# VectorE's output adds of a fused attention and FFN kernel, each moved into the step of its own product

## The chip, the cores and the metric

The kernel runs on one core of one Trainium2 chip. The metric is the device time of one execution in microseconds (us). Engines: TensorE (PE, matmuls), VectorE (DVE), ScalarE (ACT), GpSimd (POOL), and SyncE (SP), which here issues every DMA.

## The reference

All of it is float32; x is 2048 tokens by 256.

```
xn   = layernorm(x)
k, q, v = W_K xn, W_Q xn, W_V xn          # 16 heads of 128
attn = softmax(causal(q k^T) / sqrt(128))
z    = attn v                              # per head
ffn  = W2 . fwht(silu(W1 xn) * (W3 xn))
out  = x + W_O concat(z) + ffn
```

## The kernel before

The FFN and the values of all heads come first (about the first 300 us). Then the attention runs head by head, 16 times the same period of 8 steps; heads 1 to 14 are one loop body, heads 0 and 15 are written out, and a last stretch called `over` drains what is left. Each engine has its own program; the order of its work is written out by hand, and semaphores tie the engines together.

Every float32 product is made of three matmuls on a high and a low part (`_hi`, `_lo`) of each operand (L811 to L813). ScalarE copies the high part out of PSUM, and VectorE (for pt and v: GpSimd) subtracts it to get the low part.

**One step s.** A step treats two rows of 128 queries, the big one (row 15 - s) and the small one (row s); together they have 17 blocks of 128 keys. TensorE computes `scores` into PSUM banks 0 to 4. VectorE's `maxima` (L715 to L726) takes the maxima bank by bank. ScalarE's `exponential` (L529) writes exp(scores - max) to `raw` in three pieces, two of the big row and one of the small. VectorE's `transpose_blocks` (L733) transposes `raw` in 32x32 blocks, the big row first, then the small one. SP's `send` writes each row to `scratch` in DRAM with four DMAs (L275), and `bring` fetches it transposed into `pt_lo` (L289). Two steps later ScalarE's `p_to_hi` (L538) and GpSimd's `p_to_lo` (L371) split it.

**z and its output.** A chunk z of 256 queries needs the rows of two steps. TensorE's `weighted_sum` gathers it in bank 7. ScalarE copies it (`z_to_hi`, L544), VectorE subtracts (`z_to_lo`, L737), and TensorE's `output` multiplies it by W_O into one of two ring banks. VectorE's `output` (L749) then does two `scalar_tensor_tensor` of 128x256: acc = product x 1/(row sum) + acc. The ring is shared with the projections of K and Q (`kq_to_lo`, L697 and L700), in the fixed order `ITEMS`; TensorE may overwrite a bank once the reader of the item before in it is done (for an output: `out_added`).

The output chunks are numbered 0 to 7. Even steps 0, 2, 4, 6 carry the small ones (`O_SMALL`: chunks 3, 5, 7 of the head before, and 1), odd steps 1, 3, 5, 7 the big ones (`O_BIG`: chunks 4 and 6 of the head before, and 0 and 2). TensorE's order is: in an even step `scores`, small `output`, big `weighted_sum`; in an odd step `scores`, big `weighted_sum`, big `output`, small `weighted_sum`; the projections stand between them.

VectorE's order in an even step: `z_to_lo` of the small chunk, the adds of the big chunk of the step before, both `maxima`, `reciprocals`, big transpose, small transpose, `kq_to_lo`. In an odd step: the adds of the small chunk of the step before, both `maxima`, `z_to_lo` of the big chunk, big transpose, small transpose, `kq_to_lo`.

Of the kernel before, what the change touches and what calls it, by code (L numbers as in the profile page):

```python
# [18 lines left out]
def attention_ffn_kernel(nc, x, w_heads, w_values, w1t, w3t, w2t, hadamard, out):  # L19
# [19 lines left out]
    STEPS = TILES // 2  # L39
# [27 lines left out]
    O_SMALL = {0: (-1, 3), 2: (-1, 5), 4: (-1, 7), 6: (0, 1)}  # L67
    O_BIG = {1: (-1, 4), 3: (-1, 6), 5: (0, 0), 7: (0, 2)}
# [24 lines left out]
    with ExitStack() as ctx:  # L93
# [122 lines left out]
        def wait(engine, semaphore, count):  # L216

            if not isinstance(count, int) or count > 0:
                engine.wait_ge(semaphore, count)

        def kq_count(h, item):

            return 8 * h + KQ_FIRST + KQ_ITEMS.index(item) + 1
# [4 lines left out]
        def z_count(h, z):  # L228

            return CHUNKS * h + z + 1  # L230
# [363 lines left out]
        def _(dve):  # L594
# [94 lines left out]
            def ring_bank(item):  # L689
                return bank(RING_AT + ITEM[item] % RING)  # L690

            def kq_to_lo(h, item):
                which, b = item
                sl = slice(b * BANK, (b + 1) * BANK)
                dve.wait_ge(proj_hi, kq_count(h, item))
                if which == "K":
                    dve.tensor_tensor(k_lo[:, sl], ring_bank(item), k_hi[:, sl].bitcast(F32),  # L697
                                      ALU.subtract).then_inc(proj_lo, 1)
                else:
                    dve.scalar_tensor_tensor(out=q_lo[:, sl], in0=ring_bank(item), scalar=SCALE,  # L700
                                             in1=q_hi[:, sl].bitcast(F32), op0=ALU.mult,
                                             op1=ALU.subtract).then_inc(proj_lo, 1)

            def maxima(h, s, small):

                j = row_of(s, small)
                at = big_banks(s) if small else 0
                end = STEP_BANKS if small else big_banks(s)
                parts = [(b, b + 1) for b in range(at, end)]
                if not small:  # L710
                    parts[0:2] = [(0, 2)]
                for i, (a, b) in enumerate(parts):
                    n = min((b - a) * BANK, (j + 1) * P - (a - at) * BANK)
                    scores = ps[:, a * BANK:a * BANK + n]
                    dve.wait_ge(scored, STEP_BANKS * (STEPS * h + s) + b)  # L715
                    if b == end:
                        dve.memset(wait_mark[:, :], 0.0)
                        dve.tensor_tensor_reduce(  # L718
                            out=scores, in0=scores, in1=mask[:, BANK - n:], scale=1.0,
                            scalar=-3e38, op0=ALU.add, op1=ALU.max, accum_out=bank_max[:, j, i:i + 1]  # L720
                        ).then_inc(maxed, 1)
                    else:
                        dve.tensor_reduce(bank_max[:, j, i:i + 1], scores, AX_X, ALU.max).then_inc(maxed, 1)  # L723

                dve.wait_ge(maxed, 4 * (STEPS * h + s) + (4 if small else len(parts)))
                dve.tensor_reduce(neg_max[:, j:j + 1], bank_max[:, j, 0:len(parts)], AX_X, ALU.max,  # L726
                                  negate=True).then_inc(negmaxed, 1)

            def transpose_blocks(h, s, small):

                dve.wait_ge(exped, piece_count(h, s, 2 if small else 1))
                v = raw_row(s, small).rearrange("p (b k) -> p b k", k=BLK)
                dve.transpose(v, v).then_inc(blocked, 1)  # L733

            def z_to_lo(h, z):
                dve.wait_ge(z_hi_done, z_count(h, z))
                dve.tensor_tensor(z_lo[:, :], bank(Z, 0, CHUNK_Q), z_hi[:, :].bitcast(F32),  # L737
                                  ALU.subtract).then_inc(z_lo_done, 1)

            def output(h, z):  # L740

                c = Z_ORDER[z]
                dve.wait_ge(rcp_done, z_count(h, z))
                dve.wait_ge(wo_product, z_count(h, z))

                wait(dve, out_added, z_count(h, z) - 1)
                for t in range(2):
                    j = 2 * c + t
                    ins = dve.scalar_tensor_tensor(  # L749
                        out=acc[:, j, :], in0=ring_bank(("O", z))[:, t * D:(t + 1) * D], scalar=row_rcp[:, j:j + 1],  # L750
                        in1=acc[:, j, :], op0=ALU.mult, op1=ALU.add)
                ins.then_inc(out_added, 1)

            def reciprocals(h, m):

                dve.wait_ge(exped, piece_count(h, 2 * m + 1, 2))
                j, i = 2 * (CHUNKS - 1 - m), 2 * m
                dve.tensor_reduce(row_sum[:, j:j + 2], row_part[:, j:j + 2, :], AX_X, ALU.add).then_inc(summed, 1)
                dve.wait_ge(summed, CHUNKS // 2 * h + m + 1)
                dve.reciprocal(row_rcp[:, j:j + 2], row_sum[:, j:j + 2]).then_inc(rcp_done, 1)  # L760
                dve.reciprocal(row_rcp[:, i:i + 2], row_part[:, i:i + 2, 0]).then_inc(rcp_done, 1)

            def period(h, first=False, more=True, over=False):
                def absent(back):
                    return first and back or over and not back

                for s in range(6 if over else STEPS):
                    if s in O_SMALL and not absent(O_SMALL[s][0]):
                        z_to_lo(h + O_SMALL[s][0], O_SMALL[s][1])

                    back, z = (O_SMALL if s % 2 else O_BIG)[(s - 1) % STEPS]
                    if s == 0:
                        back -= 1
                    if not absent(back):
                        output(h + back, z)
                    if not over:
                        maxima(h, s, 0)
                        maxima(h, s, 1)
                    if s % 2 == 0 and not (first and s == 0) and not (over and s > 0):
                        reciprocals(*((h, s // 2 - 1) if s else (h - 1, 3)))  # L780
                    if s == 7 and more:
                        kq_to_lo(h, ("K", 0))
                    if s in O_BIG and not absent(O_BIG[s][0]):
                        z_to_lo(h + O_BIG[s][0], O_BIG[s][1])
                    if not over:
                        transpose_blocks(h, s, 0)
                    if s == 7 and more:
                        kq_to_lo(h, ("K", 1))
                    if not over:
                        transpose_blocks(h, s, 1)  # L790
                    if s < 2 and not over:
                        kq_to_lo(h, ("Q", s + 1))
                    if s == 3 and more and not over:
                        kq_to_lo(h, ("K", 3))
                    if s >= 5 and more and not over:
                        kq_to_lo(h, (("Q", 3), ("Q", 0), ("K", 2))[s - 5])

            dve.wait_ge(mask_ready, 2)
            for item in KQ_ITEMS[2:]:
                kq_to_lo(-1, item)  # L800
            period(0, first=True)
            with dve.Fori(1, HEADS - 1) as h:
                period(h)
            period(HEADS - 1, more=False)
            period(HEADS, over=True)

# [274 lines left out]
```

## Time and profile before

| what | value |
|---|---|
| median of 3 runs | 1470.24 us (1469.47 to 1470.25) |
| the profiled execution | 1468.4 us |
| its span, first to last instruction | 1466.5 us |
| mean granted TensorE clock | 0.983 of full speed |
| busy: PE, DVE, ACT, POOL | 1350.7, 1048.4, 836.4, 838.5 us |
| period of one head in the loop | 72.28 us |

The profiled execution took 1.8 us less than the median. The period is the distance of the same instruction in successive heads. Times below are us from the start of the span. In a timeline the first column is the start, the second the duration; durations of neighbours on an engine overlap a little, so what an instruction costs its engine is better read from the distance of two starts.

### The profile page before, as it was taken

To read this page: it belongs to the slowest core of one execution; us is meant where nothing else is said; L and a number is where in the kernel's file an instruction comes from. 1 tells how busy PE (TensorE), PEld (TensorE's weight loads), DVE (VectorE), ACT (ScalarE), POOL (GpSimd) and SP (SyncE) were. 2 spreads that over 40 slices of the span, in tenths; PEclk is the share of its full clock that TensorE was granted. 3 is DMA by queue.
4 is the path that set the end of the run, shared out by engine and by line. 5 is a ranking of instruction groups with operands and counts; after the bars stand their busy time and mean duration, and the time that the engine had idled before them with its cause. 6 is when DMAs were issued, how large, how long until landed. Compare 5 with 4: busy or idle time off the path is not lost.

```text
span 1466.5 us, 26458 instructions
## 1 busy us (share of the span) xinstructions
PE 1350.7 (92%) x8104; PEld 1189.0 (81%) x8104; DVE 1048.4 (71%) x2389; ACT 836.4 (57%) x1623; POOL 838.5 (57%) x532
## 2 busy tenths in 40 slices
PE   3999999969999999999999999999999999999986
PEld 2878888758888888888888888888888888888875
DVE  6643300378888888888888888888888888888882
ACT  3322244366666666666666666666666666666662
POOL 4410000065757585858585857576767676767574
PEclk7899999989999999999999999999999999999998
DMA  4100056589897978888888887978898888888885
GB/s 145 68 1 0 0 151 194 157 249 284 256 284 250 283 244 282 246 284 260 276 254 281 248 286 253 283 252 284 251 281 247 281 262 264 271 261 271 263 266 167
DMA packets 278458, 335.13 MB, mean 229 GB/s; under 512 B 62736, under 2 KB 251280, under 8 KB 273808
## 3 DMA queue, kind: packets, MB, share of 16 engines
q1 hardware_dynamic: 278416, 334.65, 73.1%
q8 instruction: 17, 0.28, 0.1%
q14 instruction: 25, 0.20, 0.0%
HBM read 173.08 MB, written 161.48 MB: 228 GB/s over the span
## 4 chain that ended last, share of the span: by engine, by line
PE 27%; issue 26%; POOL 24%; DVE 8%; ACT 6%; DMA 4%; SPq 4%; POOLq 1%; DVEq 0%; ACTq 0%
POOL pt_lo L371 21%; PE ps L811 9%; PE ps L812 9%; PE ps L813 9%; SPq L275 3%; DMA scratch<-raw 3%; ACT raw L529 3%; DVE had L723 3%; ACT pt_hi L538 1%; POOL v_lo L376 1%; DVE raw L733 1%; POOL wqk_lo L355 1%; DMA raw<-w3t 1%; DVE acc L749 1%; POOL wqk_hi L353 1%
## 5 line engine op out<-in xcount | busy, mean ns | idle before, releaser
L371 POOL TENSOR_TENSOR pt_lo<-pt_lo,pt_hi 128x640 fp32r<-128x640 f32 (+11 forms) x384 | 662.0, 1756 | 241.7 <-ACT pt_hi L538 241.7
L529 ACT ACTIVATE raw<-ps,had 128x1024 f32<-128x1024 f32 (+7 forms) x384 | 329.2, 865 | 323.0 <-DVE had L726 263.3
L733 DVE STREAM_TRANSPOSE raw<-raw 128x2048 f32<-128x2048 f32 (+15 forms) x256 | 322.0, 1292 | 94.5 <-ACT raw L529 92.3
L811 PE MATMUL ps<-pt_hi,v_hi 128*128 128x256 f32 (+1 forms) x1152 | 324.6, 282 | 20.7 <-POOL pt_lo L371 19.1
L812 PE MATMUL ps<-pt_lo,v_hi 128*128 128x256 f32 (+1 forms) x1152 | 329.6, 286 | 0.0
L813 PE MATMUL ps<-pt_hi,v_lo 128*128 128x256 f32 (+1 forms) x1152 | 327.5, 284 | 0.0
L538 ACT CAST pt_hi<-pt_lo 128x640 fp32r<-128x640 f32 (+11 forms) x384 | 282.3, 812 | 12.0 <-DMA pt_lo<-scratch 11.9
L811 PE MATMUL ps<-k_hi,q_hi 128*128 128x512 f32 (+3 forms) x640 | 238.2, 372 | 18.5 <-ACT raw L529 18.4
L723 DVE TENSOR_REDUCE had<-ps 128x1 f32<-128x1024 f32 (+1 forms) x256 | 237.9, 950 | 8.1 <-PE ps L813 8.1
L811 PEld LDWEIGHTS ps<-pt_hi,v_hi 128*128 128x128 f32 x1152 | 219.8, 191 | 29.6 <-issue 21.8
L813 PE MATMUL ps<-k_hi,q_lo 128*128 128x512 f32 (+3 forms) x640 | 233.9, 365 | 0.0
L812 PE MATMUL ps<-k_lo,q_hi 128*128 128x512 f32 (+3 forms) x640 | 233.3, 365 | 0.0
L812 PEld LDWEIGHTS ps<-pt_lo,v_hi 128*128 128x128 f32 x1152 | 219.1, 190 | 2.9
L813 PEld LDWEIGHTS ps<-pt_hi,v_lo 128*128 128x128 f32 x1152 | 221.5, 192 | 0.0
L376 POOL TENSOR_TENSOR v_lo<-v_next,v_hi 128x512 fp32r<-128x512 f32 x64 | 82.7, 1303 | 223.4 <-ACT v_hi L513 223.4
L811 PEld LDWEIGHTS ps<-k_hi,q_hi 128*128 128x128 f32 x640 | 121.2, 189 | 41.1 <-ACT raw L529 23.3
L813 PEld LDWEIGHTS ps<-k_hi,q_lo 128*128 128x128 f32 x640 | 120.9, 189 | 19.3
L812 PEld LDWEIGHTS ps<-k_lo,q_hi 128*128 128x128 f32 x640 | 121.3, 190 | 17.9
L737 DVE TENSOR_TENSOR z_lo<-ps,z_hi 128x256 fp32r<-128x256 f32 x128 | 54.2, 424 | 102.7 <-ACT z_hi L544 102.7
L718 DVE CUSTOM_DVE_ANT_0 ps<-ps,aux 128x512 f32<-128x512 f32 (+3 forms) x256 | 126.8, 495 | 0.0
L811 PE MATMUL ps<-wo_hi,z_hi 128*128 128x256 f32 x256 | 79.3, 310 | 43.6 <-DVE z_lo L737 41.6
L697 DVE TENSOR_TENSOR k_lo<-ps,k_hi 128x512 fp32r<-128x512 f32 x64 | 42.5, 664 | 101.8 <-ACT k_hi L489 101.8
(101 smaller groups left out, 2202.8 us busy)
## 6 DMA issues: line engine op xcount, KB each, us to landing
all_values<-raw SPq DMA_DIRECT2D x16, 1024.0 KB, 5.0
v_next<-all_values SPq DMA_DIRECT2D x16, 1024.0 KB, 5.4
scratch<-raw SPq DMA_DIRECT2D x64, 256.0 KB, 5.4
pt_lo<-scratch SPq DMA_DIRECT2D x16, 1024.0 KB, 5.5
scratch<-raw SPq DMA_DIRECT2D x64, 240.0 KB, 5.2
pt_lo<-scratch SPq DMA_DIRECT2D x16, 960.0 KB, 6.1
scratch<-raw SPq DMA_DIRECT2D x64, 224.0 KB, 5.4
pt_lo<-scratch SPq DMA_DIRECT2D x16, 896.0 KB, 5.0
```

What stands on the lines that cost most here:

```text
L275: sp.dma_start(to[a], raw_row(s, small)[a * BLK:(a + 1) * BLK].rearrange("k (g x) -> k g x", g=4)).then_inc(stored[small], 16)
L371: pool.tensor_tensor(lo, lo.bitcast(F32), hi.bitcast(F32), ALU.subtract).then_inc(pt_lo_done, 1)
L376: pool.tensor_tensor(v_lo[:, sl], v_next[:, sl], v_hi[:, sl].bitcast(F32), ALU.subtract).then_inc(v_lo_done, 1)
L529: act.activation(to[:, first // P:(first + n) // P], ps[:, a * BANK:a * BANK + n].rearrange("p (i g k) -> p i g k", g=4, k=BLK), ACT.Exp, ...
L538: act.copy(pt_row(pt_hi, j, a, b), pt_row(pt_lo, j, a, b).bitcast(F32)).then_inc(pt_hi_done, 1)
L718: dve.tensor_tensor_reduce(out=scores, in0=scores, in1=mask[:, BANK - n:], scale=1.0, scalar=-3e38, op0=ALU.add, op1=ALU.max, accum_out=ba ...
L723: dve.tensor_reduce(bank_max[:, j, i:i + 1], scores, AX_X, ALU.max).then_inc(maxed, 1)
L733: dve.transpose(v, v).then_inc(blocked, 1)
L737: dve.tensor_tensor(z_lo[:, :], bank(Z, 0, CHUNK_Q), z_hi[:, :].bitcast(F32), ALU.subtract).then_inc(z_lo_done, 1)
L811: pe.matmul(dst, a[0], b[0], start=start, stop=False, skip_group_check=True)
L812: pe.matmul(dst, a[0], b[1], start=False, stop=False, skip_group_check=True)
L813: return pe.matmul(dst, a[1], b[0], start=False, stop=stop, skip_group_check=True)
```

## The change

Only VectorE's order changes. The adds of a small chunk go from the start of the next (odd) step to the even step of their product, between the transposes of the big and of the small row. The adds of a big chunk go from the next (even) step, where they stood behind `z_to_lo`, to the end of their own odd step, behind both transposes and `kq_to_lo`. The last stretch `over` needs five steps in place of six. No operation is added or taken away.

```diff
-                for s in range(6 if over else STEPS):
+                for s in range(5 if over else STEPS):
                     if s in O_SMALL and not absent(O_SMALL[s][0]):
                         z_to_lo(h + O_SMALL[s][0], O_SMALL[s][1])
-
-                    back, z = (O_SMALL if s % 2 else O_BIG)[(s - 1) % STEPS]
-                    if s == 0:
-                        back -= 1
-                    if not absent(back):
-                        output(h + back, z)
                     if not over:
                         maxima(h, s, 0)
                         maxima(h, s, 1)
...
                         transpose_blocks(h, s, 0)
                     if s == 7 and more:
                         kq_to_lo(h, ("K", 1))
+                    if s in O_SMALL and not absent(O_SMALL[s][0]):
+                        output(h + O_SMALL[s][0], O_SMALL[s][1])
                     if not over:
                         transpose_blocks(h, s, 1)
...
                         kq_to_lo(h, (("Q", 3), ("Q", 0), ("K", 2))[s - 5])
+                    if s in O_BIG and not absent(O_BIG[s][0]):
+                        output(h + O_BIG[s][0], O_BIG[s][1])
```

## Rows read from the trace of the kernel before

**Rows 1.** The page, part 1: busy time of each engine.

```profile
PE 1350.7 (92%) x8104; PEld 1189.0 (81%) x8104; DVE 1048.4 (71%) x2389; ACT 836.4 (57%) x1623; POOL 838.5 (57%) x532
```

**Rows 2.** Busy time by stretch: PE, PEld, DVE, ACT, POOL, clock, DMA share, GB/s.

```profile
374.00:446.00 72.00, 68.25 (x433) 60.93 (x432) 59.62 (x139) 46.56 (x92) 49.78 (x33) 1.00 0.87 270
```

**Rows 3.** Waits from 390 to 1380 us: total, times, longest.

```profile
ACT raw L529 <- DVE had L726: 213.5, 91, 4.0
...
PE ps L811 <- DVE z_lo L737: 24.7, 26, 1.5
PE ps L811 <- POOL pt_lo L371: 12.9, 18, 0.9
...
PE ps L811 <- ACT raw L529: 8.8, 13, 0.7
```

**Rows 4.** Timeline of TensorE, one head; in brackets idle before, and releaser.

```profile
783.53 0.28 PE L813 MATMUL ps<-wo_hi,z_lo 128*128 128x256 f32 x1
...
785.03 0.45 PE L811 MATMUL ps<-k_hi,q_hi 128*128 128x512 f32 x1
...
786.24 0.39 PE L813 MATMUL ps<-k_hi,q_lo 128*128 128x512 f32 x1
...
799.57 0.38 PE L811 MATMUL ps<-wo_hi,z_hi 128*128 128x256 f32 x1 [0.46 <-DVE z_lo L737]
...
809.56 0.50 PE L811 MATMUL ps<-k_hi,q_hi 128*128 128x512 f32 x1 [0.68 <-ACT raw L529]
...
817.23 0.39 PE L811 MATMUL ps<-wo_hi,z_hi 128*128 128x256 f32 x1 [1.43 <-DVE z_lo L737]
...
825.77 0.38 PE L811 MATMUL ps<-pt_hi,v_hi 128*128 128x256 f32 x1 [0.88 <-POOL pt_lo L371]
...
1315.54 0.50 PE L811 MATMUL ps<-k_hi,q_hi 128*128 128x512 f32 x1 [0.68 <-ACT raw L529]
```

**Rows 5.** Timeline of VectorE, same head: steps 0, 1 to 2, 2 to 3.

```profile
785.73 0.42 DVE L737 TENSOR_TENSOR z_lo<-ps,z_hi 128x256 fp32r<-128x256 f32 x1 [1.23 <-ACT z_hi L544]
...
786.86 1.81 DVE L723 TENSOR_REDUCE had<-ps 128x1 f32<-128x1024 f32 x2
...
804.59 0.42 DVE L737 TENSOR_TENSOR z_lo<-ps,z_hi 128x256 fp32r<-128x256 f32 x1 [0.73 <-ACT z_hi L544]
804.93 0.87 DVE L749 SCALAR_TENSOR_TENSOR acc<-ps,had,acc 128x256 f32<-128x256 f32 x2
805.72 1.81 DVE L723 TENSOR_REDUCE had<-ps 128x1 f32<-128x1024 f32 x2
...
810.42 2.50 DVE L733 STREAM_TRANSPOSE raw<-raw 128x1792 f32<-128x1792 f32 x2 [1.14 <-ACT raw L529]
812.85 0.83 DVE L749 SCALAR_TENSOR_TENSOR acc<-ps,had,acc 128x256 f32<-128x256 f32 x2
813.61 1.81 DVE L723 TENSOR_REDUCE had<-ps 128x1 f32<-128x1024 f32 x2
```

**Rows 6.** Timelines of ScalarE (two rows) and GpSimd (one), same head.

```profile
808.30 1.11 ACT L529 ACTIVATE raw<-ps,had 128x1024 f32<-128x1024 f32 x1 [3.74 <-DVE had L726]
...
819.58 2.22 ACT L538 CAST pt_hi<-pt_lo 128x960 fp32r<-128x960 f32 x3
...
819.78 1.31 POOL L376 TENSOR_TENSOR v_lo<-v_next,v_hi 128x512 fp32r<-128x512 f32 x1 [2.66 <-ACT v_hi L513]
```

**Rows 7.** SP: waits from 374 to 1382 us, timeline, page's part 6.

```profile
SPq L289 <- PE ps L813: 20.6, 25, 1.8
...
811.29 1.19 SPq L289 DMA_DIRECT2D pt_lo<-scratch  x2
812.57 6.64 SPq L275 DMA_DIRECT2D scratch<-raw  x8
821.07 0.97 SPq L289 DMA_DIRECT2D pt_lo<-scratch  x2
...
pt_lo<-scratch SPq DMA_DIRECT2D x16, 960.0 KB, 6.1
```

## Prediction

> **What bounds the kernel now.** The page first: TensorE is busy for 92% of the span, VectorE for 71% [rows 1]. That is a mean over stages, so the second view is the busy time by stretch. In 72 us of a middle head, TensorE works 68.25 us at a granted clock of 1.00, that is at the 2.4 GHz level, while VectorE works 59.62 us [rows 2]. So at most 72 - 68.25 = 3.75 us of a head are idle time that a better order could remove. The waits of the middle heads say who ends them [rows 3]: TensorE waits for `z_lo` of VectorE (26 times), for `pt_lo` of GpSimd (18) and for the exponentials (13), about 25, 13 and 9 us over some 14 heads.
>
> The timeline of one head places these gaps [rows 4]: 0.46 us at 799.57 (big output of step 1, for `z_lo`), 0.68 at 809.56 (scores of step 3, for the exponentials), 1.43 at 817.23 (big output of step 3, for `z_lo`) and 0.88 at 825.77 (`weighted_sum` of step 4, for `pt_lo`), together 3.45 us. From there to the next head TensorE runs on almost without a gap. The period is (1315.54 - 809.56) / 7 = 72.28 us, the same for all loop heads.
>
> A head therefore has two halves. From step 4 to step 0 TensorE sets the pace. From step 0 to step 4 the path leaves it: VectorE's maxima, ScalarE's exponentials, VectorE's transposes, then maxima again. The exponential of step 2 starts after 3.74 us of waiting for VectorE's negated maximum [rows 6], and such waits hold 213.5 us over these heads [rows 3]. What makes the maxima of steps 0 to 3 start earlier shortens the head, until TensorE has no gaps left.
>
> **The price of one pair of adds.** By starts, 805.72 - 804.93 = 0.79 us [rows 5]. In the order before, the big pair stands between `z_to_lo` and the maxima of steps 0, 2, 4 and 6, the small pair in front of the maxima of steps 1, 3, 5 and 7.
>
> **The big pair, step 1 to 2.** It goes in front of `z_to_lo` of step 2, where VectorE is idle for 0.73 us, waiting for ScalarE's `z_hi` [rows 5]. The next instruction starts 0.08 us before the reported end of the adds (804.93 + 0.87 against 805.72), so the hole is 0.81 us wide by starts and the pair fits with 0.02 to spare. Its cover is ScalarE's cast; were the cover gone, it would cost its 0.79 again. The maxima of step 2 then follow `z_to_lo` directly, at its start + 0.34, and gain the whole 0.79 us. The lower bound is 0.65, if the adds had to end by their reported end (0.87 - 0.73 = 0.14 late); the upper is 0.79.
>
> **The big pair, step 7 to 0.** The hole in front of `z_to_lo` is 1.23 us, so the pair is covered. The maxima at 786.86 could start at 785.73 + 0.34 = 786.07. But they read two banks of scores, whose last matmul starts at 786.24 and takes 0.39 [rows 4, 5]: 786.63, and some hundredths for the hand-over. Gain 0.2 us, between 0 and 0.23. After that the scores are late next, and they are TensorE's own pace.
>
> **The big pairs, steps 3 to 4 and 5 to 6.** They too leave the front of the maxima. But behind 825.77 TensorE has no gap that VectorE ends until the next head [rows 4], so nobody is waiting for that time: 0, between 0 and a few tenths.
>
> **The small pairs.** Before step 3, the order was big transpose, small transpose, adds, maxima: 810.42, then 812.85 for the adds, then 813.61 for the maxima, with no idle time between them [rows 5]. Now it is big transpose, adds, small transpose, maxima. The sum in front of the maxima is the same, so they gain nothing. What moves is the end of the small transpose, 0.79 us later, and in steps 0 and 6 the Q subtraction behind it. SP issues the small row's four DMAs behind the big row's four; the eight take 6.64 us [rows 7], so the small ones begin some 3.3 us after 812.57, and the small transpose would now end near 812.92 + 0.79 = 813.7 against 815.9. Price 0. The cover is the big row's four issues.
>
> **New waits.** A pair now waits for a product of its own step. In step 7, the tightest, TensorE's product ends at 783.53 + 0.28 = 783.81, and VectorE comes free at 785.73 - 1.23 = 784.50 [rows 4, 5]. In step 1 the product begins at 799.57 and VectorE comes free at 804.59 - 0.73 = 803.86. Behind a late product would stand `z_to_lo` of the next step, and behind it TensorE's small output; I price this at 0. The ring banks come free earlier than before, but none of TensorE's gaps names them.
>
> **How the gain travels.** Step 0 brings 0.2, so exponentials, transposes and maxima of step 1 are 0.2 earlier, and the gap at 799.57 closes by 0.2. Step 2 adds 0.79: the exponential at 808.30 comes 0.99 earlier. TensorE's gap of 0.68 at 809.56 closes, since TensorE itself comes only 0.2 earlier. The chain goes on through the transposes at 810.42 and the maxima at 813.61 to `z_lo`, so the output at 817.23 is 0.99 earlier; its gap only shrinks to about 1.3 because TensorE also arrives 0.2 + 0.68 earlier. ScalarE's exponentials and v cast, and GpSimd's `v_lo` at 819.78, idle 2.66 us before it [rows 6], move too, and with them `pt_lo` and the matmul at 825.77. From there on all is TensorE's pace: a period of 72.28 - 0.99 = 71.3 us.
>
> SP must follow. The row of step 1 is fetched at 811.29, its 960 KB take 6.1 us to land, and ScalarE casts it at 819.58 [rows 6, 7]: 2.2 us of slack, of which about 0.8 is used up, since the fetch moves only by the 0.2 of step 0. SP also waits for TensorE 20.6 us in these heads [rows 7], so it is not the slowest loop.
>
> **The sum.** Big pairs of 15 heads do this (head 0 has no outputs in its first steps; head 15's first four steps have the same order): 15 x 0.99 = 14.9 us. The last stretch changes nothing I can price. The profiled execution would take 1468.4 - 14.9 = 1453.5; the median is 1.8 higher, so 1470.2 - 14.9 = 1455.4 us. With the bounds of the two terms, 15 x (0.65 + 0) = 9.8 to 15 x (0.79 + 0.23) = 15.3, and up to 0.2 a head for what steps 4 to 6 might add: 1452 to 1461 for this case.
>
> **The rivals.**
>
> *Another gate takes most of it* (0.14). VectorE's hole of step 1 is filled to 0.02 us, the DMA engines are busy for 0.87 of the time [rows 2], and the fetched row keeps 1.4 us of slack. If a wait of ScalarE for a fetched row, or of SP for a landing, takes two thirds, 5 us remain: 1465. For it: several reserves shrink at once. Against it: each is still positive.
>
> *VectorE's order is not what costs* (0.12). The same time, 1470.2. For it: VectorE has 12 us of a head idle, and TensorE is the busiest engine. Against it: three of TensorE's four gaps end at VectorE or at work behind its maxima.
>
> The Trainium skill, Perfetto Trace Analysis, section Identifying the Most-Contended Engine, would have the engine of highest occupancy optimized first, and VectorE isn't that one. By that rule the sum would be 0 and the time this rival's. This case's waits [rows 3] speak against it, as just said.
>
> *Slower: the small transpose is late for SP* (0.06). In one even step SP has finished the big row's issues before the small transpose ends, and the loop of fetch, split and `weighted_sum` hangs on it. Its price is 0.79 us in one step of 15 heads, with no gain got: 1470.2 + 11.9 = 1482. It decides from the point where the small row's first DMA is now issued less than 0.79 us after its transpose; the trace has about 3 us [rows 5, 7].
>
> *More than the forecast* (0.06): the maxima of steps 4 and 6 count as well and TensorE's gaps close further, 1.5 us a head: 1448.
>
> **How the numbers follow.** Forecast 0.62, 1455.4 us. Faster by over 0.2% (2.9 us, about what a measurement of this kernel can tell from no change): forecast, most of the first rival and the last one, 0.81; within 0.2%: 0.12; slower: 0.07. The range of 1450 to 1465 holds the forecast with its bounds and most of the partial case, and leaves out no change, slower, and more than 20 us.
>
> **What would show it.** Right: a period near 71.3 us; the adds inside the hole before `z_to_lo` in step 2, so that its idle time falls from 0.73 to about 0; maxima of step 2 starting 0.34 us after `z_to_lo`; TensorE's gap before the scores of step 3 gone, the one at the output of step 3 still near 1.3 and the one at step 4 near 0.9. Wrong: idle time of VectorE in front of the adds (the product late), or ScalarE idle before `p_to_hi` for a DMA, or SP idle for a small transpose.

## The result, and the profile after

The changed kernel takes 1457.14 us (median of 4, 1454.75 to 1457.69) against 1470.05 before (median of 4): ratio 0.991, 95% interval 0.9893 to 0.9927. Forecast were 1455.4 us and a gain of 14.9 us; measured is a gain of 12.9. The profiled execution took 1454.75 us, 13.65 less than the one before; the other three took about 2.5 us longer than it.

The period of a loop head fell from 72.28 to 71.32 us. The output of step 3 begins at 454.62 and, five heads on, at 811.22: 356.60 / 5 = 71.32. The timeline of TensorE of the changed kernel, the same gaps as in [rows 4]:

```profile
454.62 0.39 PE L809 MATMUL ps<-wo_hi,z_hi 128*128 128x256 f32 x1 [1.44 <-DVE z_lo L737]
...
794.33 0.38 PE L809 MATMUL ps<-wo_hi,z_hi 128*128 128x256 f32 x1 [0.29 <-DVE z_lo L737]
...
811.22 0.39 PE L809 MATMUL ps<-wo_hi,z_hi 128*128 128x256 f32 x1 [1.44 <-DVE z_lo L737]
...
819.73 0.39 PE L809 MATMUL ps<-pt_hi,v_hi 128*128 128x256 f32 x1 [0.88 <-POOL pt_lo L371]
```

The gap of 0.46 us is now 0.29, the one of 0.68 before the scores of step 3 is gone, and those of 1.43 and 0.88 are still there: 3.45 us became 2.61. This accounts for 0.84 of the 0.95 us that a head is shorter (the remaining 0.1 us is taken up further below). Busy time by stretch, to hold against [rows 2], has TensorE at 69.14 of 72 us:

```profile
374.00:446.00 72.00, 69.14 (x440) 61.92 (x439) 60.70 (x144) 47.17 (x93) 50.74 (x33) 1.00 0.86 265
```

The timeline of VectorE of the changed kernel, step 0, then steps 1 to 3, answers to [rows 5]:

```profile
780.66 0.42 DVE L737 TENSOR_TENSOR z_lo<-ps,z_hi 128x256 fp32r<-128x256 f32 x1 [0.45 <-ACT z_hi L544]
781.60 1.82 DVE L723 TENSOR_REDUCE had<-ps 128x1 f32<-128x1024 f32 x2 [0.51 <-PE ps L811]
...
793.77 0.42 DVE L737 TENSOR_TENSOR z_lo<-ps,z_hi 128x256 fp32r<-128x256 f32 x1
...
798.53 0.86 DVE L749 SCALAR_TENSOR_TENSOR acc<-ps,had,acc 128x256 f32<-128x256 f32 x2
799.36 0.42 DVE L737 TENSOR_TENSOR z_lo<-ps,z_hi 128x256 fp32r<-128x256 f32 x1
799.70 1.81 DVE L723 TENSOR_REDUCE had<-ps 128x1 f32<-128x1024 f32 x2
804.40 2.05 DVE L733 STREAM_TRANSPOSE raw<-raw 128x1792 f32<-128x1792 f32 x1 [1.14 <-ACT raw L529]
806.37 0.83 DVE L749 SCALAR_TENSOR_TENSOR acc<-ps,had,acc 128x256 f32<-128x256 f32 x2
807.12 0.57 DVE L733 STREAM_TRANSPOSE raw<-raw 128x384 f32<-128x384 f32 x1
807.62 1.78 DVE L723 TENSOR_REDUCE had<-ps 128x1 f32<-128x1024 f32 x2
```

In step 0 the adds have gone from between `z_lo` and the maxima, but the maxima now wait 0.51 us for scores: `z_lo` to maxima is 0.94 us, before it was 786.86 - 785.73 = 1.13, a gain of 0.19. In step 2 the adds fill the hole of 0.73 us, `z_lo` follows with no idle time, and the maxima start 0.34 us after it; before it was 1.13, a gain of 0.79. Before step 3 the small pair stands between the two transposes, and from the first transpose to the maxima it is 807.62 - 804.40 = 3.22 us, against 813.61 - 810.42 = 3.19 before.

SP, in its waits and its timeline, against [rows 7]:

```profile
SPq L289 <- PE ps L811: 8.3, 16, 1.2
SPq L275 <- DVE raw L733: 2.4, 5, 1.2
...
805.96 1.19 SPq L289 DMA_DIRECT2D pt_lo<-scratch  x2
807.24 6.59 SPq L275 DMA_DIRECT2D scratch<-raw  x8
```

The small transpose of step 2 ends at 807.69; the eight issues begin at 807.24 and take 6.59 us, so the small row's four come about 3 us later. SP's waits for a transpose are 2.4 us in all, so the later small transpose holds it up very little. SP's waits for TensorE fell from 20.6 us to 8.3: it is closer to being late.

### The profile page after: what moved, and what is told of

Same layout as the page of the kernel before. It is cut to its first block, busy times and chain, and to the rows that moved or that the text cites. A ratio compares the mean times of both kernels' runs of the same rounds, so it can differ in the third digit from the quotient of the medians.

```text
span 1452.9 us, 26444 instructions
## 1 busy us (share of the span) xinstructions
PE 1350.0 (93%) x8104; PEld 1189.3 (82%) x8104; DVE 1051.3 (72%) x2389; ACT 837.1 (58%) x1623; POOL 838.6 (58%) x532
## 4 chain that ended last, share of the span: by engine, by line
POOL 32%; issue 31%; PE 24%; DVE 6%; ACT 3%; DMA 2%; SPq 1%; POOLq 1%; DVEq 0%; ACTq 0%
POOL pt_lo L371 27%; PE ps L809 8%; PE ps L810 8%; PE ps L811 8%; POOL v_lo L376 2%; ACT raw L529 2%; DVE had L723 1%; DVE raw L733 1%; POOL wqk_lo L355 1%; DMA raw<-w3t 1%; POOL wqk_hi L353 1%; SPq L275 1%; DVE k_lo L636 1%; POOL wo_lo L355 1%; DMA scratch<-raw 1%
## 5 line engine op out<-in xcount | busy, mean ns | idle before, releaser
L733 DVE STREAM_TRANSPOSE raw<-raw 128x2048 f32<-128x2048 f32 (+15 forms) x256 | 328.6, 1299 | 94.6 <-ACT raw L529 92.0
L538 ACT CAST pt_hi<-pt_lo 128x640 fp32r<-128x640 f32 (+11 forms) x384 | 282.3, 811 | 13.3 <-DMA pt_lo<-scratch 13.1
L749 DVE SCALAR_TENSOR_TENSOR acc<-ps,had,acc 128x256 f32<-128x256 f32 x256 | 108.4, 464 | 6.0 <-PE ps L811 5.2
```

The costliest lines, as they stand in the source:

```text
L538: act.copy(pt_row(pt_hi, j, a, b), pt_row(pt_lo, j, a, b).bitcast(F32)).then_inc(pt_hi_done, 1)
L749: ins = dve.scalar_tensor_tensor(out=acc[:, j, :], in0=ring_bank(("O", z))[:, t * D:(t + 1) * D], scalar=row_rcp[:, j:j + 1], in1=acc[:, j ...
```

## The experiments

Besides each run's time stands the period, read as the distance of step 3's `z_lo` in successive loop heads of its profile.

| kernel | median us | ratio to before (95%) | period us |
|---|---|---|---|
| before | 1469.7 to 1470.1 | | 72.28 |
| changed | 1457.1 | 0.9910 (0.9893 to 0.9927) | 71.33 |
| e1_big_only | 1456.2 | 0.9914 (0.9897 to 0.9930) | 71.33 |
| e2_small_only | 1470.5 | 1.0004 (0.9994 to 1.0014) | 72.28, the first 73.41 |
| e3_big_step1 | 1458.7 | 0.9931 (0.9914 to 0.9947) | 71.48 |
| e4_big_step7 | 1466.6 | 0.9979 (0.9970 to 0.9989) | 72.07 |
| e5_big_steps35 | 1469.2 | 0.9997 (0.9988 to 1.0006) | 72.26 |
| e6_small_in_hole | 1448.3 | 0.9847 (0.9826 to 0.9868) | 70.14, some 70.8 to 72.8 |
| e7_z_lo_early | 1459.4 | 0.9936 (0.9922 to 0.9950) | 71.3, one of 71.7, three near 72.8 |
| e8_both | 1458.1 | 0.9919 (0.9904 to 0.9934) | 71.57, single 70.1, 70.7 and 73.4 |
| e9_v_cast_early | 1445.6 | 0.9846 (0.9831 to 0.9860) | 70.48, some 70.7 to 71.5 |
| e10_small_and_v | 1446.8 | 0.9843 (0.9829 to 0.9856) | 69.3 to 74.6 |

**Which pairs carry the gain.** Four kernels take the change apart. e1, the small pairs left where they were:

```diff
-                    if not absent(back):
+                    if s % 2 and not absent(back):
                         output(h + back, z)
...
+                    if s in O_BIG and not absent(O_BIG[s][0]):
+                        output(h + O_BIG[s][0], O_BIG[s][1])
```

> Only the big pairs are added in their own step; the small pairs stay at the start of the next odd step. Theory (the gain is the big pairs leaving the front of the maxima of steps 0 and 2): period 71.3 us and a time within 3 us of the full change, about 1457. Rival (small pairs carry part of it, by the ring banks that come free earlier or by the odd steps' maxima): period above 71.6, gain clearly smaller.

e2, the reverse:

```diff
-                    if not absent(back):
+                    if s % 2 == 0 and not absent(back):
...
+                    if s in O_SMALL and not absent(O_SMALL[s][0]):
+                        output(h + O_SMALL[s][0], O_SMALL[s][1])
                     if not over:
                         transpose_blocks(h, s, 1)
```

> Only the small pairs are moved, between the two transposes; the big pairs stay behind the next step's z subtraction. Theory: the sum of work in front of the odd steps' maxima is unchanged, period 72.3 us, time 1470 within 2 us. Rival 1 (the later small transpose delays SP's sends): up to 0.79 us a head slower, period 73.1, 1482. Rival 2 (the small move helps by itself): period below 72.1.

The big pairs alone give the whole gain, the small ones nothing, neither way. In 13 of 14 loop heads of e2 the later small transpose costs nothing, so the slower rival falls. The first loop head is 1.13 us longer; ScalarE waits there for two fetched rows (0.49 and 1.23 us), and whether the later transpose is the cause isn't shown.

e3, e4 and e5 move only the big pairs of step 1, of step 7, and of steps 3 and 5 (shown is e3):

```diff
+                    if (s % 2 or (s - 1) % STEPS not in (1,)) and not absent(back):
...
+                    if s in (1,) and not absent(O_BIG[s][0]):
+                        output(h + O_BIG[s][0], O_BIG[s][1])
```

> Only the big pair of step 1 is added in its own step, everything else as before the change. Theory: it brings 0.79 us in front of the maxima of step 2; period 71.5 us, time 1470.1 - 15 x 0.79 = 1458. Rival (the gain is spread over all four big pairs): about a quarter of it, period 72.0, 1467.

> Only the big pair of step 7 is added in its own step. Theory: the maxima of step 0 gain 0.2 us until the scores are late; period 72.1 us, time 1470.1 - 3 = 1467. Rival (all pairs count alike): 0.24 to 0.8 us a head, the upper end 1458.

> Only the big pairs of steps 3 and 5 are added in their own steps. Theory: behind step 4 TensorE sets the pace and nobody waits for that time; period 72.3 us, time 1470 within 2 us. Rival (these pairs count too): up to 1.5 us a head faster, 1448.

Step 1's pair brings 72.28 - 71.48 = 0.80 us a head, step 7's 0.21, those of steps 3 and 5 0.02. That settles the division: 0.80 and 0.21 against the forecast 0.79 and 0.2. Together they give 0.95 rather than 1.01; where the last 0.06 goes was not traced.

**Does the chain from step 0 to 3 set the period?** e6 puts the small pairs where VectorE waits for ScalarE:

```diff
+                    if s in O_SMALL and not absent(O_SMALL[s][0]):
+                        output(h + O_SMALL[s][0], O_SMALL[s][1])
                     if not over:
                         transpose_blocks(h, s, 0)
...
-                    if s in O_SMALL and not absent(O_SMALL[s][0]):
-                        output(h + O_SMALL[s][0], O_SMALL[s][1])
                     if not over:
                         transpose_blocks(h, s, 1)
```

> The changed kernel, but the small pairs stand in front of the big row's transpose, where VectorE waits for ScalarE (1.56 us in step 0, 1.14 in step 2), and not behind it. Theory (what counts is the work of the VectorE and ScalarE chain from step 0 to step 3, and a hole before the transpose is free): the maxima of step 3 come 0.79 us earlier; in step 0 about 0.3 us more, until ScalarE's cast of z is late for the first exponential of step 1; period 71.3 - 1.1 = 70.2 us, time 1457 - 16 = 1441. Rival 1 (another gate, SP or the fetched rows, is close behind): period 70.8 or more. Rival 2 (only the order of the big pairs matters): 71.3.

Half a hit: the period is 70.14 us in most heads, 1.19 less than with the change, but five loop heads are longer (70.79 to 72.77 us), and the median of 1448.3 (1442.5 to 1451.7) is 7 us above the forecast. The rival of another gate holds for those: in each of the five, ScalarE waits 0.92 to 1.97 us for the fetched row of step 1. The timeline of ScalarE of e6 in the longest shows it, and under it TensorE's, of the head before and of this one:

```profile
807.75 2.20 ACT L538 CAST pt_hi<-pt_lo 128x960 fp32r<-128x960 f32 x3 [1.45 <-DMA pt_lo<-scratch]
```

```profile
742.20 0.38 PE L809 MATMUL ps<-pt_hi,v_hi 128*128 128x256 f32 x1 [0.94 <-POOL pt_lo L371]
...
813.50 0.38 PE L809 MATMUL ps<-pt_hi,v_hi 128*128 128x256 f32 x1 [1.72 <-POOL pt_lo L371]
```

ScalarE waits 1.45 us for the fetched row of step 1, and TensorE's gap at step 4 grows from 0.94 to 1.72. Counted from `z_lo` of step 3, the `weighted_sum` of step 4 begins after 10.14 us in this head and after 9.06 in the head before. That is 1.1 of the 2.6 us by which this head is longer than 70.14. The rest stands behind the gap, where busy time by stretch shows a granted clock (third column from the end) below 1.00, in this loop head of e6 only:

```profile
813.50:830.00 16.50, 16.50 (x100) 15.44 (x101) 12.27 (x28) 10.99 (x23) 12.23 (x10) 0.90 0.84 269
```

What makes the fetched row late is argued and not shown. SP waits for TensorE only 0.4 us in all these heads, which fits a loop of sends and fetches that has become the pace, but no run made that loop shorter.

**Is TensorE's largest gap worth closing?** In step 3, e7 subtracts z between the two maxima, on top of the change; e8 does so on top of e6:

```diff
                     if not over:
                         maxima(h, s, 0)
+                    if s == 3 and not absent(O_BIG[s][0]):
+                        z_to_lo(h + O_BIG[s][0], O_BIG[s][1])
+                    if not over:
                         maxima(h, s, 1)
...
-                    if s in O_BIG and not absent(O_BIG[s][0]):
+                    if s in (1, 5, 7) and not absent(O_BIG[s][0]):
```

> The changed kernel, but in step 3 VectorE subtracts the big z between the maxima of the two rows, so that TensorE's largest gap (1.44 us at the output of step 3) becomes shorter by about 1.3 us. Theory: the chain through ScalarE's v cast and GpSimd's splits still ends at the same time, so that TensorE waits that much longer at step 4's weighted sum; period 71.3, time 1457 within 2. Rival (TensorE's largest gap is what its idle time costs): period 70.0, time 1438.

> Small pairs in front of the big transpose, and the big z of step 3 subtracted between the maxima of the two rows. Theory: as with the small pairs alone, period 70.2, since the second edit shortens a gap that is not on the path. Rival: with the chain shorter, TensorE's own gap at the output of step 3 binds, and both together give 69.5 or less.

e7: the gap at step 3's output falls to 0.48 us, the one at step 4 grows from 0.88 to 1.78, and the period stays 71.3, as the theory has it. But three of its heads are about 1.45 us longer, and its 1459.4 us lie just outside the forecast of 1457 within 2. In e8 nearly all are longer: 71.57 in place of the 70.2 expected, a miss of both theories. Its timeline of TensorE at step 4, first a head of period 70.08, then one of 71.56:

```profile
1175.84 0.39 PE L812 MATMUL ps<-pt_hi,v_hi 128*128 128x256 f32 x1 [1.82 <-POOL pt_lo L371]
...
1176.19 0.29 PE L814 MATMUL ps<-pt_hi,v_lo 128*128 128x256 f32 x1
1176.31 0.28 PE L812 MATMUL ps<-pt_hi,v_hi 128*128 128x256 f32 x1
...
531.54 0.38 PE L812 MATMUL ps<-pt_hi,v_hi 128*128 128x256 f32 x1 [1.74 <-POOL pt_lo L371]
...
534.93 0.41 PE L812 MATMUL ps<-pt_hi,v_hi 128*128 128x256 f32 x1
535.15 0.41 PE L813 MATMUL ps<-pt_lo,v_hi 128*128 128x256 f32 x1
```

Behind the second gap, the matmuls start 0.22 us apart and no longer 0.12. Busy time by stretch of e8, for the 13.5 us behind either gap:

```profile
1175.80:1189.30 13.50, 13.46 (x91) 12.53 (x92) 10.40 (x23) 10.39 (x23) 10.71 (x9) 1.00 0.88 275
...
531.50:545.00 13.50, 13.46 (x83) 12.73 (x84) 9.26 (x23) 9.29 (x20) 9.46 (x8) 0.87 0.90 285
```

TensorE is busy for 13.46 us in both stretches, yet in the second the mean granted clock is 0.87, so part of it ran at 1.2 GHz and not at 2.4. By the clock alone this would be about 0.13 x 13.5 = 1.8 us (an estimate from this row); the two periods differ by 71.56 - 70.08 = 1.48 us, and e7's three heads by about 1.45.

So moving 1 us of idle time from one gap into another made the kernel slower. The two gaps of 1.44 and 0.88 us of the changed kernel are followed by no lower clock in any loop head. One gap of 1.71 to 1.82 us was followed by it in 11 of 14 loop heads of e8. But one of 1.72 to 1.83 us was followed by it in only 3 of 14 of e7, and of the two heads shown the one with the longer gap kept its clock. The length of the gap alone doesn't decide, and no run shows what does. The Trainium skill, Perfetto Trace Analysis, section Matmul Optimizations, says that TensorE scales its power by utilization and that matmuls should run back to back in batches; the row with 0.87 agrees, the row with 1.00 behind a gap as long doesn't show it.

**The way into step 4.** e9 leaves VectorE as changed and moves ScalarE's v cast of step 3 to the start of the step:

```diff
+                    if s == 3 and not over:
+                        v_to_hi(h, 2)
                     if s in (1, 3) and not absent(O_BIG[s][0]):
                         z_to_hi(h + O_BIG[s][0], O_BIG[s][1])
...
-                    for b in [] if over else V_AT.get(s, []):
+                    for b in [] if over or s == 3 else V_AT.get(s, []):
```

> The changed kernel, but ScalarE casts the v block of step 3 at the start of the step, in an idle time of 1.4 us, instead of behind the exponentials. Theory (the path into step 4's weighted sum runs through ScalarE's v cast and GpSimd's two splits, not through TensorE's output gap of step 3): the gap of 0.88 us at the weighted sum closes and the period falls from 71.33 to about 70.5 us, 1445. Rival (the fetched row of step 1 or SP's loop is close behind): ScalarE then waits for the fetched row, and the period stays above 70.9.

A hit: 70.48 us and 1445.6. From its waits between 390 and 1360 us:

```profile
PE ps L811 <- DVE z_lo L739: 22.8, 27, 1.5
...
PE ps L811 <- POOL pt_lo L371: 3.6, 10, 1.0
```

TensorE's waits for `pt_lo` fell to 3.6 us, from 12.9 before the change [rows 3] and 13.1 in the changed kernel, while the larger ones for `z_lo` stayed. In five of the 14 loop heads the period is 0.2 to 1.0 us longer, and in four of these ScalarE waits 0.4 to 0.9 us for a fetched row: the rival holds in part.

e10 joins e6 and e9.

> The small pairs in front of the big transposes and the early v cast together. Theory (the fetched row of step 1 is now the gate, since SP's loop of sends and fetches leaves ScalarE waiting up to 2 us in some heads): little beyond the small pairs alone, 70.1 us where the row is in time, with some longer heads, 1440 to 1449. Rival (the chain through ScalarE and GpSimd still sets it): 69.3 us, 1433. A third outcome, from the runs before: a gap of TensorE longer than about 1.5 us at step 4 is followed by a lower granted clock and costs about 1.4 us more in that head.

The median lies within the theory's 1440 to 1449 and is e9's within the intervals. By heads it is neither alone: the fastest reach the rival's 69.3, others 70.5 to 74.6. The third outcome came too, in the heads of 72.3 and 74.6 us: behind gaps of 1.62 and 1.72 us at step 4 the granted clock falls to 0.66 and 0.50 over 5 us. It is no rule, though, for e7 has gaps up to 1.83 us without it. Its waits of ScalarE and SP, where the changed kernel has 0.9 and 8.3:

```profile
ACT pt_hi L538 <- DMA pt_lo<-scratch: 19.8, 16, 2.6
...
SPq L289 <- PE ps L813: 1.4, 2, 0.8
```

In the four heads of 69.0 to 69.4 us ScalarE doesn't wait for the fetched row of step 1, in the other ten it waits 0.7 to 2.6 us for it: the fetched rows are now what binds. e6, e9 and e10 all beat both kernels, the one before by 1.5%, the changed one by 0.6 to 0.8%; among them this study doesn't separate a best one, though e9 varies least (1445.3 to 1449.8).

## Why the prediction was right

- **What bounds the kernel:** right. From step 0 to 4 the path runs through VectorE and ScalarE; shortening it shortened every head, and time saved behind step 4 (e5) was worth 0.02 us. One reading the prediction left out: the profile puts 59.7 us of the exponentials' waits down to the landing of a send and not to the maxima. The landing didn't hold those of steps 0 and 1: in e4, where only the big pair of step 7 moved, they came 0.19 us earlier with the maxima, counted from the start of step 4.
- **Big pair, step 1 to 2:** forecast 0.79 us, 0.79 in the timeline, 0.80 alone in e3. The hole of 0.73 us held the pair.
- **Big pair, step 7 to 0:** forecast 0.2, 0.19 in the timeline, 0.21 in e4; then the scores were late, as said.
- **Small pairs:** forecast 0, e2 0.00 us in 13 of 14 heads. The cover by the big row's four issues held.
- **New waits for a product:** no idle time stands in front of any pair in any loop head, only in the last stretch from 1419.68 us on (0.80 to 1.80 us). From the output of step 3 of head 15 (1394.98 before, 1381.40 after) to the end it is 71.5 us in both kernels, so the last stretch is worth nothing, as priced.
- **TensorE's gaps:** the scores' gap closed and that of step 4 stayed, as said. The gap of step 3 was to be 1.3 and is 1.44. The first matmul after the gap at 809.56 starts 0.33 us ahead of the next (809.56 to 809.89), others 0.23, and that 0.1 us went with the gap, so TensorE arrives 0.1 earlier at the next one; the sum had left it out.
- **The sum:** mis-sized by a little. Forecast 0.99 us a head, measured 0.95 to 0.96: 15 heads give 14.4. The profiled execution gained 13.65, because its head 0 stood 0.55 us later than before's already in its first scores, before any output, and 0.12 us more by the end of head 0. The other three executions are some 2.5 us longer than the profiled one, and those of e1 0.7 to 1.8; without a profile of them it stays open where.
- **The rival of another gate** had 0.14. It does not show in the change (ScalarE's waits for fetched rows are 0.9 us in all), but it is real and close: the prediction left that row 1.4 us of slack, and the wait appeared when 1.2 us more were taken (e6).
- **The rival by the rule of the busiest engine** falls: VectorE, at 71% against TensorE's 92%, was where the time was. By the section of the Trainium skill named ahead, as the prediction read it, the gain would have been 0; here it was 0.9%. The section names the engine to optimize first and no gain, so the 0 was the prediction's reading; VectorE's order paid because TensorE's gaps hung on it.

## What to carry to other kernels

Work that nobody waits for belongs into a hole in front of a wait, not between a late wait and what the next engine needs; whether it stands in its own step is beside the point (e2 and e5 moved pairs into their own step and gained nothing, while e6 gains 0.6% more by another place within the same step). Size the gain by the part of the period in which the path leaves the busiest engine: the same 0.79 us was worth 0.80 in one step, 0.21 in another and 0.02 in two together. Don't go by the largest gap of the busiest engine: e7 shortened it and won nothing (by the medians it lost 2 us, with intervals that just touch), e9 left it and closed the smaller one at step 4, by a cast on the path into it, and won 0.8%.

## What was not expected of the hardware

Idle time of TensorE that is gathered in one place can cost more than itself. Of the 34 loop heads of e6, e7, e8 and e10 in which TensorE had a gap of 1.62 to 1.83 us at step 4, 17 show a lower granted clock right behind it (e8 11 of 14, e7 3 of 14, e10 2 of 3, e6 1 of 3). In the head of e8 shown, with TensorE otherwise over 99% busy, it was 0.87 over the next 13.5 us, in part at 1.2 GHz, and such a head took about 1.5 us more. In the kernel before and the changed one, with gaps up to 1.46 and 0.89 us some eight us apart, no loop head shows a clock below 1.00. Why gaps of the same length go either way stays open.
